# A chunked delta-rule attention stage: the next chunk's gram moved to the end of a step, and copies and a scaling moved to ScalarE

## The reference

```
def step(S, inp):
    q_t, k_t, v_t, beta_t, alpha_t = inp
    S = S * alpha_t[..., None, None]
    kv = jnp.einsum('bhk,bhkv->bhv', k_t, S)
    S = S + jnp.einsum('bhk,bhv->bhkv', k_t, (v_t - kv) * beta_t[..., None])
    o_t = jnp.einsum('bhk,bhkv->bhv', q_t, S)
    return (S, o_t)
...
o = o * lax.rsqrt(var + EPS) * norm_w
o = o * (z * jax.nn.sigmoid(z))
out = jnp.einsum('btv,hv->bth', o.reshape(b_, t_, VAL_DIM), out_w)
```

## Time and profile before

| | us |
|---|---|
| median of three runs | 8394.17 |
| the three runs | 8395.7, 8381.44, 8394.17 |
| the profiled execution, its own time | 8398.92 |
| span of its records | 8397.2 |
| stretch that holds the stage of the change | 1044 to 2609 |

### The profile page before, as it was taken

How to read it: one execution, slowest core, us unless ns; L and a number is a source line. 1 busy time by engine, 2 the same in 40 slices (tenths; PEclk the granted TensorE clock), 3 DMA queues, 4 the chain that set the end, 5 groups by cost and what they waited for, 6 DMA issues and landing times. The chain is left out here.

```text
span 8397.2 us, 277296 instructions
## 1 busy us (share of the span) xinstructions
PE 7016.8 (84%) x120944; PEld 4988.1 (59%) x120944; DVE 5867.6 (70%) x10703; ACT 4051.7 (48%) x6730; POOL 2918.4 (35%) x2152
## 2 busy tenths in 40 slices
PE   7999699999996997998997997998998779445566
PEld 3444478888885665665665665665665556345444
DVE  6665389999996885885885885885786657752366
ACT  3554145555553774774774775775775312210121
POOL 0101033333333773773773773773773000001000
PEclk8999599999998999998998998999999889555556
DMA  0000000000001221221221221221221000000000
GB/s 14 1 1 1 3 6 4 4 4 4 4 3 37 73 68 43 70 71 42 70 71 40 71 70 42 71 69 41 70 73 32 0 16 1 3 3 4 5 0 13
DMA packets 192003, 255.70 MB, mean 30 GB/s; under 512 B 59957, under 2 KB 86452, under 8 KB 189876
## 3 DMA queue, kind: packets, MB, share of 16 engines
q1 hardware_dynamic: 190772, 237.70, 10.7%
HBM read 27.84 MB, written 2.10 MB: 4 GB/s over the span
## 5 line engine op out<-in xcount | busy, mean ns | idle before, releaser
L1759 PE MATMUL wa_front<-w_wqkv,wa_xsT 128*128 128x512 f32 x2000 | 995.5, 621 | 39.5 <-PEq L66 20.4
L1681 POOL TENSOR_TENSOR XNT<-XNT 128x1024 f32<-128x1024 f32 x396 | 937.6, 2368 | 253.4 <-DVE XNT L1865 253.4
L1684 POOL TENSOR_TENSOR XNT<-XNT,wa_rnorm 128x1024 f32<-128x1024 f32 x330 | 627.9, 1903 | 364.5 <-DVE wa_rnorm L1873 364.5
L1862 DVE TENSOR_TENSOR XNT<-wa_front,w_scaled 128x1024 f32<-128x1024 f32 x330 | 393.6, 1193 | 309.9 <-ACT wa_sq L1700 228.0
L1759 PEld LDWEIGHTS wa_front<-w_wqkv,wa_xsT 128*128 128x128 f32 x2000 | 346.4, 193 | 317.7 <-issue 296.9
L446 PE MATMUL a0h_ring<-a0h_QT,a0h_KT 32*128 32x512 f32 (+3 forms) x1536 | 457.4, 567 | 14.2 <-ACT a0h_E L564 10.4
L564 ACT ACTIVATE a0h_E<-a0h_ring 128x512 f32<-128x512 f32 (+1 forms) x640 | 320.6, 554 | 296.7 <-PE a0h_ring L446 295.4
L1700 ACT ACTIVATE wa_sq<-wa_front 128x1024 f32<-128x1024 f32 x335 | 340.4, 1016 | 181.6 <-PE wa_front L1759 181.6
L1865 DVE TENSOR_TENSOR XNT<-wa_front,w_scaled 128x512 f32<-128x512 f32 x660 | 421.5, 680 | 0.0
L1878 DVE TENSOR_REDUCE wa_norm<-wa_sq 128x16 f32<-128x1024 f32 x330 | 399.0, 1209 | 0.0
L1765 PEld LDWEIGHTS wa_front<-consts,XNT 128*128 128x128 f32 x2640 | 297.7, 142 | 124.0 <-issue 56.7
(11 more groups left out here) (636 smaller groups left out, 18302.9 us busy)
## 6 DMA issues: line engine op xcount, KB each, us to landing
wa_v_look<-wa_v_all SPq DMA_DIRECT2D x990, 128.0 KB, 2.4
wa_v_look<-wa_v_all SPq DMA_DIRECT2D x660, 64.0 KB, 2.0
wal_v_look<-wal_v_all SPq DMA_DIRECT2D x198, 128.0 KB
wal_v_look<-wal_v_all SPq DMA_DIRECT2D x132, 64.0 KB
w_wqkv<-in_L_ffn_Wqkv_dram SPq DMA_DIRECT2D x6, 1024.0 KB, 6.5
w_wo<-in_L_ffn_Wo_dram SPq DMA_DIRECT2D x6, 512.0 KB, 7.2
w_wqkv<-in_L_ffn_Wqkv_dram SPq DMA_DIRECT2D x12, 256.0 KB, 7.9
f2w_raw<-in_L_ffn_w_dram SPq DMA_DIRECT2D x48, 64.0 KB, 1.9
```

The source lines that it names most:

```text
L1681: g.tensor_tensor(rot[:, at], rot[:, at], part[:, at], ALU.add).then_inc(s[summed], 1)
L1684: g.tensor_tensor(rot[:, at], rot[:, at], spread(rnorm[:, at, :], HDW), ALU.mult).then_inc(s[done], 1)
L1759: last = pe.matmul(front[:, first + i, :], xsT[:, slot, :], wqkv[:, (2 * n + i) * 512:(2 * n + i + 1) * 512], start=True, stop=True)
L1862: v.tensor_tensor(rot[:, n], src, cos, ALU.mult)
```

## The change

Five things, all in `delta_chunk_steps`:

1. The gram of a chunk, N and Nc are made one step earlier, at the end of the step in which the chunk is j: PE's gram between zt(6) and tx(6), DVE's N before x6, ACT's Nc as the last thing of a step (before `keep_weights`).
2. POOL's two `lev` instructions become the first ones of a step, ahead of `xs` and `newS`.
3. The four copies of `place()` go from DVE to ACT, two after T64b and two after the eviction of zt(6).
4. The scaling of y goes from one DVE instruction to four ACT ones with a scale operand; DVE keeps the reciprocal, now after grow(4).
5. tx(5) reads the diagonal blocks from XTc and no longer from XT, so it doesn't wait for `place()`; tx(6) and u wait for it instead.

```
 PE, tx(5)
-                        pe.wait_ge(s["x4_ready"], q + 1)
+                        pe.wait_ge(s["X_ready"], LD * q + 5)
-                            last = pe.matmul(bank[2][hi, b, 0:32], XT[hi, v, b, hi], Zt[hi, b, :], start=True, stop=True)
+                            last = pe.matmul(bank[2][hi, b, 0:32], XTc[hi, b, :], Zt[hi, b, :], start=True, stop=True)
...
 PE, start of a step
-                if q is not None:
-                    kq = conv[:, q % 3, K]
-                    pe.wait_ge(s["conv_ready"], 2 * q + 1)
-                    if q >= 1:
-                        pe.wait_ge(s["AT_ready"], q)
-                    pe.wait_ge(s["raw_copied"], 2 * q + 1)
-                    four_of(bank[0], lambda b: kq[:, b, :], lambda b: kq[:, b, :], s["gram_ps"])
...
 PE, end of a step
                 zt(6)
+                if j is not None:
+                    kq = conv[:, j % 3, K]
+                    pe.wait_ge(s["conv_ready"], 2 * j + 1)
+                    if j >= 1:
+                        pe.wait_ge(s["AT_ready"], j)
+                    pe.wait_ge(s["raw_copied"], 2 * j + 1)
+                    four_of(bank[0], lambda b: kq[:, b, :], lambda b: kq[:, b, :], s["gram_ps"])
                 if q is not None:
                     tx(6)
...
 ACT, end of a step (Nc at its start is taken out)
                     a.activation(T64[quarter(1), :, 0:32], bank[2][quarter(1), :, 0:32], ACT.Copy).then_inc(s["T64b_ready"], 1)
+                    if q >= 2:
+                        a.wait_ge(s["u_ps"], q - 1)
+                    place((2, 3))
                     a.wait_ge(s["z_ps"], q + 1)
                     a.activation(gatez[:, q % 2], bank[5][:], ACT.Tanh, scale=0.5).then_inc(s["tanh_ready"], 1)
                 evict_z(6)
+                place((0, 1))
+                if r is not None:
+                    a.wait_ge(s["gated"], r + 1)
+                    a.wait_ge(s["rstd_ready"], r + 1)
+                    for b in range(G):
+                        last = a.activation(y[:, b, :], y[:, b, :], ACT.Copy, scale=rstd[:, b:b + 1])
+                    last.then_inc(s["y_ready"], 1)
+                if j is not None:
+                    a.wait_ge(s["N_ready"], j + 1)
+                    if j >= 1:
+                        a.wait_ge(s["lev_ready"], j)
+                    for n in range(4):
+                        last = a.activation(Nc[quarter(n)], N[quarter(n), :, quarter(n)], ACT.Copy)
+                    last.then_inc(s["Nc_ready"], 1)
...
 POOL, start of a step (the same lines after newS are taken out)
+                if q is not None:
+                    g.wait_ge(s["Nc_ready"], q + 1)
+                    if q >= 1:
+                        g.wait_ge(s["zt_ps"], LZ * q)
+                        g.wait_ge(s["X_ready"], LD * q)
+                    g.tensor_tensor(lev[:, 0], Nc[:], small[:, 0:1, :].broadcast_to(tiny), ALU.mult).then_inc(s["lev0_ready"], 1)
+                    g.tensor_tensor(lev[:, 1:SMALL], Nc[:].unsqueeze(1).broadcast_to([P, SMALL - 1, G, 32]),
+                                    small[:, 1:SMALL, :].unsqueeze(2).broadcast_to([P, SMALL - 1, G, 32]),
+                                    ALU.mult).then_inc(s["lev_ready"], 1)
                 if j is not None:
                     if j >= 2:
                         g.wait_ge(s["z_ps"], j - 1)
...
 DVE
+                if r is not None:
+                    v.wait_ge(s["std_ready"], r + 1)
+                    v.reciprocal(rstd[:], std[:]).then_inc(s["rstd_ready"], 1)
                 convolve(1, 2, T0)
...
+                if j is not None:
+                    v.wait_ge(s["gram_ps"], j + 1)
+                    v.wait_ge(s["strict_ready"], j + 1)
+                    v.tensor_tensor(N[:], bank[0][:], Estrict[:], ALU.mult).then_inc(s["N_ready"], 1)
+                if q is not None:
                     v.wait_ge(s["x_ps"], LX * q + 6)
                     v.tensor_copy(XT[0:64, slot, :, 64:P], bank[4][0:64, :, 0:64]).then_inc(s["x6_ready"], 1)
-                if r is not None:
-                    v.wait_ge(s["std_ready"], r + 1)
-                    chain(v.reciprocal(rstd[:], std[:]))
-                    v.tensor_tensor(y[:], y[:], spread(rstd[:], P), ALU.mult).then_inc(s["y_ready"], 1)
```

More of the change, by code:

```diff
@@ L963, in delta_chunk_steps @@
                 "gatez_ready qk_ps AT_ready kS_ps qS_ps qS_used R_ready u_ps u_ready uend_ready o_ps o_done s_ps "
-                "loaded scaled w_ps w_ready newS_ready s_used msq_ready std_ready y_ready yT_ps yT_ready out_ps added chain")
+                "loaded scaled w_ps w_ready newS_ready s_used msq_ready std_ready gated rstd_ready y_ready yT_ps yT_ready out_ps added chain")
     K, T0 = 0, TAPS - 1
@@ L1091, in tx @@
                                 last = pe.matmul(bank[4][quarter(lo), b, 0:32], Zt[quarter(hi), b, :],
-                                                 XT[quarter(hi), v, b, quarter(hi)], start=True, stop=True)
+                                                 XTc[quarter(hi), b, :], start=True, stop=True)
                         last.then_inc(s["x_ps"], 1)
                     else:
+                        pe.wait_ge(s["x4_ready"], 2 * q + 1)
                         pe.wait_ge(s["x5_ready"], q + 1)
@@ L1151, in _ @@
                     pe.wait_ge(s["R_ready"], r + 1)
+                    pe.wait_ge(s["x4_ready"], 2 * r + 2)
                     pe.wait_ge(s["x6_ready"], r + 1)
@@ L1241, in evict_z, with place @@
                         a.activation(Zt6[64:P], bank[1][64:P, :, 0:64], ACT.Copy).then_inc(s["zt_ready"], 1)
+                def place(quarters):
+                    if q is None:
+                        return
+                    for k in quarters:
+                        last = a.activation(XT[quarter(k), q % 2, :, quarter(k)], XTc[quarter(k)], ACT.Copy)
+                    last.then_inc(s["x4_ready"], 1)
                 def keep_raw(n, at):
@@ L1249, in keep_raw @@
                     a.activation(hist[:, n, :, T0:], bank[at][:], ACT.Copy).then_inc(s["raw_copied"], 1)
[L1251 to L1257, removed]
                 if e is not None:
@@ L1322, in _ @@
                     g.tensor_tensor(newS[:], S[:], spread(of_chunk(decays[:, 2], r), P), ALU.mult).then_inc(s["newS_ready"], 1)
[L1323 to L1331, removed]
                 if j is not None:
@@ L1387, in grow @@
                     v.transpose(flat(T[:]), flat(XTc[:])).then_inc(s["T_ready"], 1)
[L1389 to L1397, removed]
                 if r is not None:
@@ L1410, in _ @@
                     v.wait_ge(s["lev0_ready"], q + 1)
+                    if q >= 1:
+                        v.wait_ge(s["x4_ready"], 2 * q)
                     v.tensor_tensor(XTc[:], lev[:, 0], ident, ALU.add).then_inc(s["X_ready"], 1)
@@ L1446, in _ @@
                     v.wait_ge(s["o_done"], r + 1)
-                    v.tensor_tensor(y[:], o[:], gatez[:, r % 2], ALU.mult)
+                    v.tensor_tensor(y[:], o[:], gatez[:, r % 2], ALU.mult).then_inc(s["gated"], 1)
                 grow(3)
@@ L1450, in _ @@
                 grow(4)
-                if q is not None:
-                    place()
+                if r is not None:
+                    v.wait_ge(s["std_ready"], r + 1)
+                    v.reciprocal(rstd[:], std[:]).then_inc(s["rstd_ready"], 1)
                 convolve(1, 2, T0)
```

## The result

The changed kernel takes 8549.11 us (median of four runs), the kernel before 8390.29 beside it: a ratio of 1.0192, 95% interval 1.0175 to 1.021. It is slower, as forecast, but by 159 us and not by 84, and lies outside the range (8425 to 8510).

The account below looks back on a forecast made before the run. PE bounds most of a step, DVE's chain the stretch from zt(6) to zt(1). There +1.60 us, elsewhere -0.35, so +1.25 over 62 steps, +78, plus 7 for turned weights: +84, 8478 us beside 8394.17; range 8425 to 8510.

Parts of the forecast that it names:

- kS, tx(6) and the gram: PE after zt(6): gram at 0.60, tx(6) at 1.69, kS at 2.29 us, where kS stood at 2.76 before.
- ACT's chain: ACT after Zt(6) at 1.11: place copies to 1.76, scaled y to 3.06, Nc to 4.34 us behind zt(6).
- lev held up by DVE: POOL's lev meets DVE's R and ga, is slowed by the shared port, and ends 6.79 us behind zt(6).
- The second step's row: Earlier profile's second step, where lev met R and ga: done 2.68 us after R's start, rest of lev 1.71 instead of 1.26.
- rawK: PE's rawK waits for POOL's xs, starting 7.43 us behind zt(6) instead of 5.83; zt(1) at 10.26 instead of 8.66, +1.60.
- First part of a step: From zt(1) to the next zt(6): tx(5) earlier and fewer small waits, -0.35 us, 15.26 to 14.91.
- Turned weights: In the 14 steps that turn weights, kS some 0.4 later, costing about 0.5 us each, +7 in all.
- The sum of these: Whole kernel: +1.25 us in each of 62 steps, +78, and +7 for turned weights, together +84 with rounding.
- zt(1) follows rawK by 0.86 + 1.97 = 2.83: On PE, zt(1) starts 2.83 us after rawK, taken from the earlier timeline and kept after the new wait.
- the last sentence: Signs of being wrong: xs ended before 6.1, Nc let lev pass before R, or PE's gaps took the clock off 1.00.
- xs in time: Rival: POOL's xs done by 4.96, zt(1) at 7.79, a step gains 1.22 us, 76 in all, 8318; chance 0.05.

Follow-up runs that it names:

- e2: Changed kernel with five extra sets of transposes of k on PE in the gap before rawK, results overwritten: 8457.05 us, ratio to before 1.0091.
- e8: Changed kernel with two extra sets of transposes of k on PE in the gap before rawK: 8466.78 us, ratio to before 1.0097.
- e1: Changed kernel with POOL's old order put back, xs and newS ahead of lev: 8321.9 us, ratio to before 0.9932.
- e10: Changed kernel with one added PE wait, transposes of k waiting for DVE's ga, which splits the idle gap: 8554.98 us, ratio to before 1.0203.
- e9: Changed kernel with the four matmuls of dt done twice, far from the gap before rawK: 8613.64 us, ratio to before 1.0264.
- e4: Kernel before with only POOL's two lev instructions moved ahead of xs and newS: 8585.56 us, ratio to before 1.0242.

## Why the prediction was wrong

The side, the mechanism of the wait and its place were right; a term of the sum was missing.

- *kS, tx(6) and the gram*: 2.29, 1.69, 0.60 behind zt(6) forecast; 2.30, 1.69, 0.60 measured.
- *ACT's chain*: Nc's end at 4.34 forecast, 4.22 measured (1931.85 + 1.25). The Trainium skill (page ScalarE: Activation LUTs, section Rules for kernel authors) has a budget of some 0.3 us for an ACTIVATE and 0.83 ns for an element, by which Nc's end was estimated at 5.2. The four scaled copies took 1.28, as in the earlier trace rows, so the rows were the better guide.
- *lev held up by DVE*: end forecast at 6.79, measured at 6.90 (1934.07 + 1.71). The second step's row was the right price. The Trainium skill (page SBUF — State Buffer, section Who interferes with whom) says that a DVE instruction with two SBUF inputs contends with a GpSimd one that reads SBUF, and that contention for the shared port pair is an exclusive lock. The trace agrees: 1.71 instead of 1.26.
- *rawK*: forecast 7.43, measured 7.57; with the clock at 1.00 zt(1) at 10.42 for 10.26 (1515.31 against zt(6) at 1504.89).
- *First part of a step*: 14.91 forecast, and 14.92 in a step at full clock (zt(1) at 1515.31 to zt(6) at 1530.23).
- *Turned weights*: 0.5 more in each of 14 steps, 7 us in all, were forecast. They didn't come: rawK stands at 7.51 there, and such a step takes 25.27 at full clock, no longer than a plain one (25.34).
- *The sum of these*: +84 forecast, +90 measured. It is as near as that partly by luck, as the 7 us too many stood against a rawK 0.14 too early. e2 and e8, which keep the wait and have no fall of the clock, lie at 8457 and 8467, inside the range.
- *What failed*: "zt(1) follows rawK by 0.86 + 1.97 = 2.83", the pitch at full clock, put behind 2.4 us of idle time. I named the clock in the last sentence only, as something that would make me wrong, without a price or a chance. The runs showed zt(1) at 4.11 behind rawK in the slow steps, and 72 us in all, nearly as much as the wait. That there is such a cost could have been read: in the first step with a q, behind its 3.83 us wait, rawK lasted 1.58 where it else takes 1.02. That row stood in the argument, and I read just its wait. That 2.4 us are enough for it, no row of before shows.
- *xs in time* (8318 forecast as a rival): not what the change did, but e1 shows what it is worth, 63 us less than before where the rival had 76. That its 8321.9 is so near 8318 is in part luck, as the kernel before took 8384.83 beside it and not 8394.17.

Left open: why about one step in four keeps the full clock behind the same gap, and what exactly of PE's work counts, that of the last few us or its share of a step. The runs show that splitting the idle time doesn't help (e10), that work inside it does (e2, e8), and that work elsewhere, which lengthens the step, doesn't (e9).

## What to carry to other kernels

When an instruction that waits is moved up in an in-order queue, list what it now stands in front of, and ask of each when its reader wants it. Here a copy of 0.6 us, which the edit left as it was and only put behind lev, stopped PE in every step, and putting it back ahead turned +1.9% into -0.7%. And when a new wait opens an idle stretch on PE, price what follows it at the lower clock as well; useless matmuls inside the stretch are a quick test of that.

## What the runs showed of the hardware

An idle 2.35 us on PE (1.9 in four of the steps), once in some 26 us, was enough to bring the granted clock down in thirteen of eighteen steps, for a loss of 1.4 to 1.7 us in each; 1.49 us (e8) brought it down in no step. Two idle stretches of 1.13 and 1.03 us, with 0.63 us of work between them, acted like one. More PE work in the gap made the kernel faster by 1%. A DVE multiply of 128x512 with two inputs in SBUF took 1.54 us beside POOL's newS and 0.69 without it (e4).
